# A two-layer graph network: joined attributes, places read at once, a difference on TensorE, one-hots in two parts

## The chip, the cores and the metric
The kernel runs on one core of one Trainium2 chip. The metric is the device time of one execution in microseconds (us). The engines are PE (TensorE), PEld (its weight loads), DVE (VectorE), ACT (ScalarE), POOL (GpSimd) and SP (SyncE, which only issues DMAs here).

## The reference
6250 nodes with 128 features, 106,250 edges sorted by target (a self loop for each node among them). Two layers, each behind a layer norm and a relu, each added to x:

```
# layer 0: attention for each of the 128 channels by itself
a  = f_src[src] + f_dst[dst];  e = where(a >= 0, a, 0.2 * a)
ex = exp(e - segment_max(e, dst)[dst])
out0 = segment_sum(f_v[src] * ex / segment_sum(ex, dst)[dst], dst)
# layer 1: a message, and one weight for each edge (softmax over ALL edges, mean of 8 heads)
scale = mlp(edge_attr_32);  msg = silu(h[src] @ W_node * scale + edge_attr_16 @ W_sh)
alpha = softmax(mlp([h[src][:64], h[dst][:64], edge_attr_32]), axis=0).mean(heads)
out1 = layernorm(h + segment_sum(msg * alpha, dst) @ W_out)
```
Inputs and outputs are float32.

## The kernel before
The sorted edges are cut into 464 pieces of at most 256, each of which belongs to one block of 128 target nodes; two pieces make a **unit** (512 edges), and there are NI = 232 units. For each piece a table in SBUF (`items_row`, int32) holds two places: where its edges begin (off) and at which row its block begins (row); so a unit has four places, side by side.

The stages run one after the other, each a block of instruction streams for the five engines, which meet at its end: `prepare` (table of places, first projections), `layer0_edges`, `node_tables` (quotient, norm, second projections), `layer1_edges`, `layer1_aggregate`, `finish`. The order within a stream is written out by hand; streams wait for each other through semaphores. `run_items` makes a loop of 29 **turns** of eight steps each (U = 8); the first and last turn are written out, the others are a hardware loop. A step works on several units at once: `f(lap, u, d)` is the part f for the unit d places ahead of the step's own.

**The join.** Layer 1 reads, for a unit, 80 rows of one array `ea_d` in DRAM: the 32 attributes twice, and the 16. `prepare` makes it at the end of ACT's stream (L538 to L541) with five DRAM to DRAM copies, in rows of 834 values (3336 bytes); SP in layer 1 waits for the five (`joined`).

**Layer 0's loop** (L790 to L1125), per unit: SP reads the four places with four `value_load`s and issues four loads (marks `lo` and rows of the target block `fd`, two each); it waits until the unit eight before is through (`hold`). POOL gathers 4 x 128 source rows (L856) into G, up to eight units ahead. ACT takes the absolute value of the marks; DVE compares them to one-hots (L1027). PE's `front` (L880, L885) turns G and adds the target part in PSUM; ACT's `bring` copies that to SBUF (L955); DVE's leaky step (L1036). The segment maximum comes from two scans on DVE (`running` L1047, then `back` L1060, backwards), which carry the last column to the next unit through ACT's `link`. DVE's `gap` (L1074) subtracts the maximum, ACT's `exps` (L977) takes exp of 513 columns, PE's `turn` transposes the one-hots (L901) and the result (L908), ACT copies both out (L988, L998), DVE's `weigh` multiplies by the gathered values (L1086) and PE's `collect` sums over edges (16 products, L926). Two units later DVE scales the one node that the unit shares with those before (`scale`, L1100, by column 0 of exp's result) and adds the two halves into SBUF at places that it reads with two `value_load`s (`add`, L1113). DVE's order in a step: leaky(1), scale(-2), running(1), add(-2, first), back(1), add(-2, second), weigh(0), gap(1), onehot(3).

**Layer 1's loop** (L1130 to L1515), per unit: SP reads four places again, then waits for PE's product of four units before (`a1p`) and of eight before (`sh_ready`), then issues six loads (L1222 to L1224). PE's `first` (L1265, L1272, which needs DVE's one-hots L1431, and these the six loads), `inputs`, `attributes`, `second`, `third`, `heads`; ACT's silus; DVE's message.

**Aggregation** (L1520 to L1671), per unit: SP loads the messages, eight units ahead; ACT (3 or 4 parts) and DVE (the odd part, every second unit, L1653) multiply by the weights; DVE makes the one-hot `pick` (512 columns, L1646) two units ahead; PE multiplies (8 products, L1604); DVE adds the two halves (L1667), each at a place that it reads just before. DVE's order: add(0, first), weigh(2) (pick and multiply), add(0, second). The two adds of neighbouring pieces may hit the same columns, so each waits for the one before it (`acc_done`).

Of the kernel before, what the change touches and what calls it, by code (L numbers as in the profile page):

```python
# [20 lines left out]
RADD = bass.bass_isa.ReduceOp.add  # L21

# [76 lines left out]
def build(nc, x, src_pad, dst_pad, ea32, ea16, w0cat, b0cat, w1cat, fc1, b1, fc2, b2, fc3, b3, w_sh,  # L99
          aw1e, ab1, aw2, ab2, aw3, ab3, w_out, out):  # L100
    top = ExitStack()
    with top:
# [17 lines left out]


# [4 lines left out]
        JOINS = (2 * EA + SH) // SH  # L126
# [13 lines left out]
        ident_b = sb("ident_b", [P, P], BF16)  # L140
        local = sb("local", [P, NI * TJ], F32)
# [227 lines left out]
        def prepare():  # L369
# [5 lines left out]
            with st:  # L375
# [60 lines left out]
                with nc.Block() as block:  # L436
# [74 lines left out]
                    def _(act):  # L511
# [26 lines left out]
                        for k in range(JOINS):  # L538
                            rows = ea16 if k == JOINS - 1 else ea32[k * SH % EA:k * SH % EA + SH, :]
                            act.dma_start(ea_d[k * SH:(k + 1) * SH, :].rearrange("a (k e) -> (a k) e", e=EQ),  # L540
                                          rows.rearrange("a (k e) -> (a k) e", e=EQ)).then_inc(joined, 16)  # L541

                    @block.vector
                    def _(dve):
# [62 lines left out]
                        nc.vector.tensor_copy(ident_b[:, :], ident[:, :])  # L607
                        dve.wait_ge(s_w, 32)
# [170 lines left out]
        def layer0_edges():  # L779

            st = ExitStack()
            with st:
# [6 lines left out]
                qe_t = sb("l0_qe", [P, 2, 2, IT + 1], F32, st)  # L789
                q_t, e_t = (qe_t[:, :, k, :] for k in range(2))  # L790
                top_t = sb("l0_top", [P, 2, IT + 1], F32, st)
                w_t = sb("l0_w", [P, R, IT + 2], F32, st)
# [17 lines left out]
                gap_ready = sem("l0_gap_ready", st)  # L810
                w_ready = sem("l0_w_ready", st)
# [9 lines left out]
                with nc.Block() as block:  # L821
                    @block.sync
                    def _(sp):
                        def rows(lap, u, d):
# [3 lines left out]
                            off = [sp.value_load(items_row[0:1, bass.ds(i * 4 + 2 * h, 1)], min_val=0, max_val=OFF_MAX) for h in range(2)]  # L828
                            row = [sp.value_load(items_row[0:1, bass.ds(i * 4 + 2 * h + 1, 1)], min_val=0, max_val=NB * P) for h in range(2)]
# [8 lines left out]

                        def step(lap, u):
                            rows(lap, u, 0)  # L840
                        run_items(sp, step)

# [22 lines left out]
                    def _(pe):  # L865
# [23 lines left out]
                        def turn(lap, u, d):  # L889
# [7 lines left out]
                            wv = w_t[:, g, 1:IT + 1].rearrange("p (j e) -> p j e", j=TJ)  # L897
# [112 lines left out]
                    def _(dve):  # L1010
# [52 lines left out]
                        def gap(lap, u, d):  # L1063

                            i, s, lp = item(lap, u, d)
                            if not exists(i, NI):
                                return
# [763 lines left out]
```

## Time and profile before

| | us |
|---|---|
| median of 3 runs (3906.5 to 3914.71) | 3909.83 |
| profiled execution | 3906.95 |
| its span | 3905.1 |

| engine | busy us | share |
|---|---|---|
| PE | 2844.4 | 73% |
| DVE | 2471.9 | 63% |
| POOL | 1931.8 | 49% |
| ACT | 1884.0 | 48% |

The stages don't overlap, so the shares of the whole span say little: the tables by stage in the rows below are what to read. "Granted clock" is the share of TensorE's full 2.4 GHz that it was given in a stretch; 0.50 is 1.2 GHz. The DMA share is the mean busy share of the core's 16 DMA engines.

### The profile page before, as it was taken

How to read it: one execution, taken by the hardware profiler on the slowest of the kernel's cores; microseconds unless marked ns; L12 is line 12 of the kernel's file. 1: busy time of each engine (PE TensorE's matmuls, PEld its weight loads, DVE VectorE, ACT ScalarE, POOL GpSimd, SP SyncE). 2: the span in 40 equal slices, each digit the busy share in tenths (PEclk: the TensorE clock that was granted, in tenths of full speed). 3: DMA queues.
4: the chain of work that ended last, by engine and by line, in shares of the span. 5: the costliest groups of instructions: out<-in, count | busy, mean ns of one | idle time of the engine just before them, and what ended most of it. 6: DMA issues, size and time to landing. Idle time of an engine off the chain costs nothing. (4 is left out here: it accounts for less than half of the span.)

```text
span 3905.1 us, 86777 instructions
## 1 busy us (share of the span) xinstructions
PE 2844.4 (73%) x18862; PEld 2202.3 (56%) x18862; DVE 2471.9 (63%) x5010; ACT 1884.0 (48%) x3923; POOL 1931.8 (49%) x1957
## 2 busy tenths in 40 slices
PE   1506666666666666646999999999999997676765
PEld 0206666666666666523666666666665664565654
DVE  5509999999999999982444444444444444655556
ACT  6205555445454554443554454554554554545454
POOL 0117777777777777405565566665665662000001
PEclk9759999999999999967999999999999998777777
DMA  3695555545455555225676677676766675344442
GB/s 72 203 322 152 147 146 144 147 144 147 142 148 145 145 146 146 78 67 160 202 202 196 198 199 200 203 203 201 203 198 195 202 203 150 111 116 117 115 118 58
DMA packets 509335, 624.22 MB, mean 160 GB/s; under 512 B 78873, under 2 KB 387605, under 8 KB 508502
## 3 DMA queue, kind: packets, MB, share of 16 engines
q1 hardware_dynamic: 372038, 272.23, 25.6%
q0 software_dynamic: 89088, 243.39, 21.8%
q10 hardware_dynamic: 48016, 106.86, 7.9%
q14 instruction: 173, 1.42, 0.1%
q8 instruction: 20, 0.33, 0.0%
HBM read 534.78 MB, written 121.55 MB: 168 GB/s over the span
## 5 line engine op out<-in xcount | busy, mean ns | idle before, releaser
L1245 POOL DMA_INDIRECT l_G<-rows_d,l_sidx x928 | 885.9, 955 | 542.1 <-DVE l_msg L1454 274.5
L856 POOL DMA_INDIRECT l_G<-rows_d,l_sidx x928 | 996.2, 1073 | 307.7 <-issue 232.0
L1431 DVE TENSOR_SCALAR l_oht<-l_lo,mine_bc 128x256 bf16<-128x256 bf16 x464 | 116.2, 305 | 765.9 <-DMA l_in<-ea_d 764.4
L880 PE MATMUL l_A<-ident,l_G 128*128 128x128 f32 x928 | 165.2, 305 | 551.4 <-DVE l_oht L1027 551.2
L1604 PE MATMUL ag_accp<-ag_msg,ag_pick 128*128 128x128 f32 x1856 | 363.8, 358 | 182.2 <-DVE ag_msg L1653 81.4
L926 PE MATMUL l_accp<-l_ohe,H 128*128 128x128 f32 x3712 | 468.9, 282 | 0.0
L1375 ACT ACTIVATE l_h<-l_H,l_cols 128x512 f32<-128x512 f32 x464 | 318.2, 686 | 296.9 <-PE l_H L1282 219.0
L926 PEld LDWEIGHTS l_accp<-l_ohe,H 128*128 128x128 f32 x3712 | 451.9, 199 | 0.0
L1604 PEld LDWEIGHTS ag_accp<-ag_msg,ag_pick 128*128 128x128 f32 x1856 | 312.5, 255 | 233.6 <-DVE big L1667 156.1
L880 PEld LDWEIGHTS l_A<-ident,l_G 128*128 128x128 f32 x928 | 106.3, 150 | 594.6 <-DVE l_oht L1027 343.4
L1587 ACT ACTIVATE ag_msg<-ag_msg,ag_alpha 128x128 f32<-128x128 f32 x812 | 261.3, 390 | 254.3 <-DMA ag_msg<-msg_d 243.1
L1311 PEld LDWEIGHTS l_SC<-big,l_h 128*128 128x128 f32 x1856 | 249.0, 198 | 143.5 <-issue 143.5
L1393 ACT ACTIVATE l_msg<-l_msg 128x512 f32<-128x512 f32 x232 | 145.7, 628 | 379.9 <-DVE l_msg L1457 379.3
L1047 DVE TENSOR_TENSOR_SCAN l_qe<-l_lo,l_qe 128x512 f32<-128x512 bf16 x232 | 298.2, 1285 | 0.3
L1720 POOL TENSOR_TENSOR fi_O<-fi_O,X 128x1280 f32<-128x1280 f32 x5 | 14.4, 2883 | 570.7 <-DVE fi_O L1778 570.7
L977 ACT ACTIVATE l_w<-l_w 128x513 f32<-128x513 f32 x232 | 146.7, 632 | 284.3 <-DVE l_w L1074 284.3
L955 ACT ACTIVATE l_qe<-l_A 128x512 f32<-128x512 f32 x232 | 138.6, 597 | 298.7 <-PE l_A L885 298.7
L1060 DVE TENSOR_TENSOR_SCAN l_top<-l_lo,l_qe 128x513 f32<-128x513 bf16 x232 | 282.5, 1218 | 0.1
L1323 PE MATMUL l_SHP<-l_win,l_in 16*128 16x128 f32 x1856 | 279.2, 291 | 0.0
L1294 PE MATMUL l_H<-l_h,big 128*128 128x512 f32 x464 | 277.8, 683 | 0.0
L1667 DVE TENSOR_TENSOR big<-big,ag_accp 128x128 f32 x464 | 133.6, 288 | 219.1 <-DVE big L1667 121.8
L1282 PE MATMUL l_H<-l_in,l_win 32*128 32x512 f32 x464 | 268.5, 659 | 0.0
(186 smaller groups left out, 6027.4 us busy)
## 6 DMA issues: line engine op xcount, KB each, us to landing
msg_d<-l_msg ACTq DMA_DIRECT2D x232, 256.0 KB
ag_msg<-msg_d SPq DMA_DIRECT2D x232, 256.0 KB, 2.6
l_fd<-dst_d SPq DMA_DIRECT2D x464, 96.0 KB
l_pd<-dst_d SPq DMA_DIRECT2D x464, 96.0 KB
l_in<-ea_d SPq DMA_DIRECT2D x464, 80.0 KB
ea_d<-in_ea_dram ACTq DMA_DIRECT2D x5, 6672.0 KB, 68.6
l_G<-rows_d,l_sidx POOLq DMA_INDIRECT x1856
l_lo<-mark_d SPq DMA_DIRECT2D x464, 64.0 KB
```

The costliest lines, as they stand in the source:

```text
L856: nc.gpsimd.indirect_dma_start(out=G[:, s, j, :], out_offset=None, in_=rows_d[0][:, :], in_offset=bass.IndirectOffsetOnAxis(ap=sidx[:, hal ...
L880: nc.tensor.matmul(av[:, j, :], G[:, s, j, 0:C], ident[:, :], is_transpose=True, start=(j == 0), stop=False, skip_group_check=True)
L926: last = nc.tensor.matmul(accp[b][:, h, k, :], we_t[:, b, h * HJ + j, k * C:(k + 1) * C], oh_e[:, b, h * HJ + j, :], start=(j == 0), stop= ...
L1047: nc.vector.tensor_tensor_scan(q_t[:, b, 1:IT + 1], lo_t[:, s, 0:IT], e_t[:, b, 1:IT + 1], q_t[:, 1 - b, IT:IT + 1], ALU.min, ALU.max).the ...
L1060: nc.vector.tensor_tensor_scan(top_t[:, b, ::-1], lo_t[:, s, IT::-1], q_t[:, b, ::-1], FAR, ALU.min, ALU.max).then_inc(top_ready, 1)
L1245: nc.gpsimd.indirect_dma_start(out=G[:, s, j, :], out_offset=None, in_=rows_d[1][:, :], in_offset=bass.IndirectOffsetOnAxis(ap=sidx[:, hal ...
L1282: nc.tensor.matmul(H1[:, :], w_in[OF_H, :], in_t[OF_H, s, :], start=True, stop=True).then_inc(h1p, 1)
L1294: nc.tensor.matmul(H2[:, :], w_fc2[:, :], h1_t[:, b, :], start=True, stop=True).then_inc(h2p, 1)
L1323: last = nc.tensor.matmul(SP_[:, j, :], sv[:, j, :], w_in[OF_SH, :], start=True, stop=True)
L1375: nc.scalar.activation(out_t[:, s % 2, :], in_p[:, :], ACT.Silu, bias=cols[:, col:col + 1]).then_inc(ready, 1)
L1587: nc.scalar.activation(mine, mine, ACT.Copy, scale=al[:, bass.ds(i * TJ + j, 1)]).then_inc(shared, 1)
L1604: last = nc.tensor.matmul(accp[b][:, h, :], pick[:, b, j, :], msg_t[:, s, j, :], start=(j % HJ == 0), stop=(j % HJ == HJ - 1))
```

## The change
Four edits.
1. `places` reads a unit's four places with one read of 16 bytes, on SP in both layers' loops, and on DVE (layer 0 and the aggregation), where it takes the place of the two reads for the adds.
2. The five joining copies leave `prepare`. SP's stream in layer 0's loop issues two DMAs for each unit, behind the unit's loads, which join SHARE = 460 columns (80 rows of 1840 bytes); a last pair takes the 32 columns that are left. `joined` is waited for as before.
3. `gap` and `exps` go. PE adds four products of the maximum with minus the identity to the transposed e in PSUM, and ACT takes exp as it copies from there. The one column that `scale` needs is a small exp of its own on ACT (`carry`). e and q are now kept for four units (R = 4) and not for two, w_t goes, and `back` waits for PE's and ACT's use of the maximum of two units before.
4. In the aggregation `pick` is made in two instructions of 256 columns, one behind each add; the read of the next unit's places stands ahead of the second add.

```diff
+        def places(engine, i):
+            _, (off_a, row_a, off_b, row_b) = nc.values_load_multi_w_load_instructions(
+                items_row[0:1, bass.ds(i * 4, 4)], engines=(engine,), min_val=0, max_val=OFF_MAX, ...
+            return (off_a, off_b), (inside(row_a), inside(row_b))
-        JOINS = (2 * EA + SH) // SH
+        SHARE = EP // NI
+        JOINS = 2 * NI + 2
...
-                        for k in range(JOINS):
-                            rows = ea16 if k == JOINS - 1 else ea32[k * SH % EA:k * SH % EA + SH, :]
-                            act.dma_start(ea_d[k * SH:(k + 1) * SH, :].rearrange("a (k e) -> (a k) e", e=EQ),
-                                          rows.rearrange("a (k e) -> (a k) e", e=EQ)).then_inc(joined, 16)
+                        nc.vector.tensor_scalar(minus[:, :], ident[:, :], -1.0, None, ALU.mult)
...  layer 0, SP
-                            off = [sp.value_load(items_row[0:1, bass.ds(i * 4 + 2 * h, 1)], ...) for h in range(2)]
-                            row = [sp.value_load(items_row[0:1, bass.ds(i * 4 + 2 * h + 1, 1)], ...) for h in range(2)]
+                            off, row = places(SP_ENGINE, i)
+                        def join(a, n):
+                            sp.dma_start(ea_d[0:2 * EA, bass.ds(a, n)].rearrange("(r a) e -> r a e", r=2),
+                                         ea32[:, bass.ds(a, n)].unsqueeze(0).to_broadcast([2, EA, n])).then_inc(joined, 16)
+                            sp.dma_start(ea_d[2 * EA:2 * EA + SH, bass.ds(a, n)], ea16[:, bass.ds(a, n)]).then_inc(joined, 16)
                         def step(lap, u):
                             rows(lap, u, 0)
+                            if exists(i, NI):
+                                join(i * SHARE, SHARE)
...  layer 0, PE
-                            pe.wait_ge(w_ready, i + 1)
+                            pe.wait_ge(top_ready, i + 1)
                             for j in range(TJ):
-                                last = nc.tensor.matmul(W[b][:, j, :], wv[:, j, :], ident[:, :], is_transpose=True,
-                                                        start=(j == 0), stop=(j == TJ - 1), skip_group_check=True)
+                                nc.tensor.matmul(W[b][:, j, :], ev[:, j, :], ident[:, :], is_transpose=True,
+                                                 start=(j == 0), stop=False, skip_group_check=True)
+                            for j in range(TJ):
+                                last = nc.tensor.matmul(W[b][:, j, :], tv[:, j, :], minus[:, :],
+                                                        start=False, stop=(j == TJ - 1), skip_group_check=True)
...  layer 0, ACT
-                            act.wait_ge(gap_ready, i + 1)
-                            nc.scalar.activation(w_t[:, g, 0:IT + 1], w_t[:, g, 0:IT + 1], ACT.Exp).then_inc(w_ready, 1)
+                            nc.scalar.activation(front_t[:, g:g + 1], top_t[:, s % 2, 0:1], ACT.Exp, scale=-1.0,
+                                                 bias=e_t[:, g, 0:1]).then_inc(front_ready, 1)
-                            nc.scalar.activation(we_t[:, b, :, 0:C], W[b][:, :, :], ACT.Copy).then_inc(we_ready, 1)
+                            nc.scalar.activation(we_t[:, b, :, 0:C], W[b][:, :, :], ACT.Exp).then_inc(we_ready, 1)
                         def step(lap, u):
-                            exps(lap, u, 0)
                             bring(lap, u, 2)
+                            carry(lap, u, 0)
                             weights(lap, u, 0)
...  layer 0, DVE
+                            if after(i, 2):
+                                dve.wait_ge(wt_ready, i - 1)
+                                dve.wait_ge(front_ready, i - 1)
                             nc.vector.tensor_tensor_scan(top_t[:, b, ::-1], lo_t[:, s, IT::-1], q_t[:, g, ::-1], ...
-                            nc.vector.tensor_tensor(w_t[:, g, 0:IT + 1], e_t[:, b, :], top_t[:, b, :],
-                                                    ALU.subtract).then_inc(gap_ready, 1)
                             running(lap, u, 1)
-                            add(lap, u, -2, 0)
+                            at = places(DVE_ENGINE, i)[1] if exists(i, NI) else None
+                            add(lap, u, -2, 0, at)
                             back(lap, u, 1)
-                            add(lap, u, -2, 1)
+                            add(lap, u, -2, 1, at)
                             weigh(lap, u, 0)
-                            gap(lap, u, 1)
                             onehot(lap, u, 3)
...  layer 1, SP: off, row = places(SP_ENGINE, i) for the four value_loads
...  aggregation, DVE
-                            nc.vector.tensor_tensor(pick[:, b, :, :], iota_row[:, :].unsqueeze(1).to_broadcast([P, TJ, P]), ...
+                            nc.vector.tensor_tensor(pick[:, b, h * HJ:(h + 1) * HJ, :], ...
                         def step(lap, u):
-                            add(lap, u, 0, 0)
+                            if u == 0:
+                                at[0] = where_to(lap, 0)
+                            add(lap, u, 0, 0, at[0])
+                            picks(lap, u, 2, 0)
                             weigh(lap, u, 2)
-                            add(lap, u, 0, 1)
+                            follows = where_to(lap, u + 1) if u + 1 < U else None
+                            add(lap, u, 0, 1, at[0])
+                            at[0] = follows
+                            picks(lap, u, 2, 1)
```

## Rows read from the trace of the kernel before
**Rows 1.** Busy time by stretch: start:end, us, then engines, granted clock, DMA share, GB/s.
```profile
174.00:269.00 95.00, 0.00 (x0) 0.00 (x0) 12.52 (x3) 0.20 (x1) 29.32 (x31) 0.50 0.99 331
...
286.90:1640.00 1353.10, 925.64 (x7818) 854.63 (x7818) 1244.92 (x2300) 679.75 (x1384) 975.77 (x924) 0.93 0.51 143
1814.00:3284.00 1470.00, 1375.76 (x8515) 925.83 (x8514) 643.44 (x1491) 742.35 (x1154) 878.21 (x942) 0.95 0.69 200
3324.00:3842.00 518.00, 363.84 (x1856) 312.48 (x1856) 299.09 (x812) 261.32 (x812) 0.00 (x0) 0.76 0.40 114
```
**Rows 2.** Timeline, start of layer 0 (start, us, engine, line); last, a DMA issue group.
```profile
167.37 3.38 ACTq L540 DMA_DIRECT2D ea_d<-in_ea_dram  x5
...
186.99 0.07 DVE L1012 MEMSET l_lo<- 128x16 bf16 x1
188.05 23.98 SPq L837 DMA_DIRECT2D l_fd<-dst_d  x1
...
286.92 0.69 DVE L1036 SCALAR_TENSOR_TENSOR l_qe<-l_qe 128x512 f32<-128x512 f32 x1
...
ea_d<-in_ea_dram ACTq DMA_DIRECT2D x5, 6672.0 KB, 68.6
```
**Rows 3.** Timeline of DVE, one unit of layer 0's loop.
```profile
1014.18 0.69 DVE L1036 SCALAR_TENSOR_TENSOR l_qe<-l_qe 128x512 f32<-128x512 f32 x1
...
1017.93 0.69 DVE L1086 TENSOR_TENSOR H<-H,l_G 128x512 f32<-128x512 f32 x1
1018.54 0.69 DVE L1074 TENSOR_TENSOR l_w<-l_qe,l_top 128x513 f32<-128x513 f32 x1
1019.14 0.47 DVE L1027 TENSOR_SCALAR l_oht<-l_who,mine_bc 128x256 bf16<-128x256 bf16 x2
1019.53 0.68 DVE L1036 SCALAR_TENSOR_TENSOR l_qe<-l_qe 128x512 f32<-128x512 f32 x1
```
**Rows 4.** Timeline of PE, ACT and DVE, one unit of layer 0's loop.
```profile
1007.12 0.77 DVE L1086 TENSOR_TENSOR H<-H,l_G 128x512 f32<-128x512 f32 x1 [0.71 <-issue]
...
1008.98 0.66 PE L880 MATMUL l_A<-ident,l_G 128*128 128x128 f32 x4 [0.49 <-DVE l_oht L1027]
...
1010.35 0.61 PE L908 MATMUL l_W<-ident,l_w 128*128 128x128 f32 x4
...
1010.79 1.95 PE L926 MATMUL l_accp<-l_ohe,H 128*128 128x128 f32 x16
...
1010.99 0.60 ACT L998 ACTIVATE H<-l_W 128x512 f32<-128x512 f32 x1
```
**Rows 5.** Groups by line, POOL's gathers in layer 0: busy, mean ns, idle before them.
```profile
L856 POOL DMA_INDIRECT l_G<-rows_d,l_sidx x928 | 996.2, 1073 | 307.7 <-issue 232.0 <-DVE H L1086 52.7 <-POOL l_sidx L853 23.1
```
**Rows 6.** Timeline of SP, layer 1: one unit's loads and the next unit's first.
```profile
2340.32 0.33 SPq L1222 DMA_DIRECT2D l_lo<-code_d  x1
...
2342.94 0.33 SPq L1224 DMA_DIRECT2D l_in<-ea_d  x1
2346.33 0.34 SPq L1222 DMA_DIRECT2D l_lo<-code_d  x1
```
**Rows 7.** Layer 1: a wait in total, one such wait, granted clock behind it.
```profile
PE l_A L1272 <- DVE l_oht L1431: 97.0, 73, 6.2
...
2373.81 0.83 PE L1272 MATMUL l_A<-l_oht,l_pd 128*128 128x256 bf16 x6 [1.74 <-DVE l_oht L1431]
...
2376.00:2378.00 2.00, 2.00 (x6) 1.26 (x6) 0.00 (x0) 1.09 (x2) 1.39 (x3) 0.50 0.58 127
```
**Rows 8.** Timeline of the aggregation: adds and a pick on DVE, products on PE.
```profile
3563.65 0.29 DVE L1667 TENSOR_TENSOR big<-big,ag_accp 128x128 f32 x1 [0.66 <-DVE big L1667]
3563.85 0.68 DVE L1646 TENSOR_TENSOR ag_pick<-iota_row,local 128x512 f32<-128x512 f32 x1
...
3565.84 0.29 DVE L1667 TENSOR_TENSOR big<-big,ag_accp 128x128 f32 x1 [0.65 <-DVE big L1667]
...
3611.87 2.07 PE L1604 MATMUL ag_accp<-ag_msg,ag_pick 128*128 128x128 f32 x8 [1.17 <-DVE ag_pick L1646]
```

More of the change, by code:

```diff
@@ L21 @@
 RADD = bass.bass_isa.ReduceOp.add
+SP_ENGINE = mybir.EngineType.SP
+DVE_ENGINE = mybir.EngineType.DVE
 P = 128
@@ L119, in dram, with inside @@
             return nc.dram_tensor(name, shape, dt).ap()
+        def places(engine, i):
+            _, (off_a, row_a, off_b, row_b) = nc.values_load_multi_w_load_instructions(
+                items_row[0:1, bass.ds(i * 4, 4)], engines=(engine,), min_val=0, max_val=OFF_MAX,
+                skip_runtime_bounds_check_because="the table on the chip is clamped to the arrays when it is built")
+            def inside(v):
+                return nc.s_assert_within(v, 0, NB * P,
+                                          skip_runtime_bounds_check_because="blocks are counted up to NB when the table is built")
+            return (off_a, off_b), (inside(row_a), inside(row_b))
         chunk_d = dram("chunk_d", [HG * P], F32)
@@ L952, in bring @@
                             act.wait_ge(a_ready, i + 1)
-                            if after(i, 2):
-                                act.wait_ge(gap_ready, i - 1)
-                            nc.scalar.activation(e_t[:, s % 2, 1:IT + 1], A[s % 2][:, :], ACT.Copy).then_inc(a_copied, 1)
+                            if after(i, R):
+                                act.wait_ge(wt_ready, i - R + 1)
+                            nc.scalar.activation(e_t[:, s % R, 1:IT + 1], A[s % 2][:, :], ACT.Copy).then_inc(a_copied, 1)
                         def link(lap, u, d):
@@ L961, in link, with carry @@
                                 return
[L962 removed]
                             act.wait_ge(q_ready, i + 1)
[L964 to L967 removed]
+                            if after(i, R - 1):
+                                act.wait_ge(front_ready, i - R + 2)
+                            nc.scalar.activation(qe_t[:, (s + 1) % R, :, 0:1],
+                                                 q_t[:, s % R, IT:IT + 1].unsqueeze(1).to_broadcast([P, 2, 1]),
                                                  ACT.Copy).then_inc(linked, 1)
[L970 removed]
+                        def carry(lap, u, d):
                             i, s, lp = item(lap, u, d)
@@ L1213, in rows @@
                                 return
-                            off = [sp.value_load(items_row[0:1, bass.ds(i * 4 + 2 * h, 1)], min_val=0, max_val=OFF_MAX) for h in range(2)]
-                            row = [sp.value_load(items_row[0:1, bass.ds(i * 4 + 2 * h + 1, 1)], min_val=0, max_val=NB * P) for h in range(2)]
+                            off, row = places(SP_ENGINE, i)
                             if after(i, R):
@@ L1522, in layer1_aggregate @@
             SHARED = [sum(OWN[0:s + 1]) for s in range(U)]
-            PICKED = [sum(1 + TJ - n for n in OWN[0:s + 1]) for s in range(U)]
+            PICKED = [sum(2 + TJ - n for n in OWN[0:s + 1]) for s in range(U)]
             st = ExitStack()
@@ L1636, in _, with picks @@
                         al = alpha[:, (HEADS - 1) % 2, :]
-                        def weigh(lap, u, d):
+                        def picks(lap, u, d, h):
                             i, s, lp = item(lap, u, d)
```

73 lines of the change are left out of this document (34 added, 39 removed).

## The prediction
> **What bounds the kernel now.** I read the times by stage first, because no single engine is busy all the way: the page puts PE at 73% and DVE at 63% of the span. [rows 1] gives four stretches: 95 us in which PE does nothing and the DMA engines are 0.99 busy; layer 0's loop, 1353.1 us, DVE busy 1244.9 of it (92%), PE 68%; layer 1's loop, 1470 us, PE busy 1375.8 (94%), DVE 44%; the aggregation, 518 us, where no engine passes 71%. Each has its own limit.
>
> *Start of layer 0* [rows 2]: ACT issues five copies that join the attributes at 167.4 us, in front of the block's end. SP's small loads for the first units then take up to 23.98 us to issue. DVE's zeroing is over at 187.06 us, but the first leaky step runs at 286.92. The limit is the joining copies, whose data layer 0 never reads.
>
> *Layer 0's loop*: the timeline of DVE over one unit [rows 3] has no idle time; a unit takes 1019.53 - 1014.18 = 5.35 us. The mean over the loop is 1353.1/231 = 5.86, since DVE idles 108 us, 3.7 us at each turn of eight units.
>
> *Layer 1's loop*: PE is nearly full, but the timeline of SP [rows 6] shows who paces it. SP starts a unit's six loads at 2340.32 and the next unit's at 2346.33: 6.01 us, of which the six issues take 2340.32 to 2343.27 = 2.95 and the other 3.06 hold four reads of places and two waits. The list of waits has no wait of SP on a product in this loop, so SP isn't held back by anyone: it is the pace. PE feels it [rows 7]: 97.0 us of waiting for the one-hots, which wait for the loads; and after a wait of 1.74 us the granted clock drops to 0.50 (1.2 GHz) for some 7 us.
>
> *Aggregation* [rows 8]: add, pick, (multiply,) add. The add at 3563.65 was idle 0.66 us behind the add before it, though that takes only 0.29: between them stands a read of a place into a register, and nothing is queued to cover it.
>
> **The change, part by part.** The sum is made against the profiled execution, 3906.95 us (span 3905.1, 1.85 around it); the median of the runs is 3909.83, 2.9 above.
>
> *Joining moved into layer 0's loop.* Without the copies at the front, the first leaky step follows the zeroing after the one-hots (0.5 us), PE's front (1008.98 to 1010.35 = 1.4 at full clock [rows 4], double at 1.2 GHz) and ACT's copy (0.6): some 4 us. The block also ends earlier by ACT's 3.38 us of issuing. 187.06 - 3.4 + 4 = 188 against 286.92: **-99 us**. Nothing else holds it: loads and gathers issue from about 170. Bounds: -95 (the stretch with idle PE) to -105.
> The price is paid in the loop. SP issues two more DMAs per unit, each 0.33 us and some 0.5 from start to start (2.95/6): 1.0 us, while three reads go. SP is held by DVE in this loop, so this lies beside. On the engines: the join is 5 x 6672 KB = 34.2 MB [rows 2], which at the 331 GB/s of the first stretch [rows 1] is 103 us of all 16 engines, or 1650 engine-us. Spread over all 16 that is 0.08 of the loop on top of 0.51, and loads are issued eight units ahead. I cost it at 15 us; 0 and, if it falls on few engines, the rival below are the ends.
>
> *Layer 0's difference on TensorE.* The subtraction (L1074) goes: the next instruction now starts 0.60 us after it (1018.54 to 1019.14) [rows 3], and DVE has no idle: 231 x 0.60 = -139 us if nothing else is late. PE gets four f32 products of 128x128; sixteen take 1.95 us (L926) [rows 4], so 0.49 a unit. PE's unit is now 1008.98 to 1012.74 = 3.76; 4.25 is under DVE's new 4.75. The dependent chain: front's start to the start of ACT's weights is 1008.98 to 1010.99 = 2.01, to become 2.50, plus an Exp of about 0.63; ready 3.13 us after front. DVE comes to its weighted product 1017.93 - 1014.18 = 3.75 after leaky, about 3.6 after front: hidden by about 0.5 us at full clock. Once a turn it is not: at 1007.12 that instruction already waits 0.71 us at the low clock, and the four products then cost twice, 0.98: 28 x 1.0 = +27. ACT loses a 0.63 us Exp and gains one of one column (0.2): off the path. The new waits of back (wt_ready, front_ready, two units old) have been met a step before; behind them on DVE only its own next add queues.
> POOL is next in line: its 928 gathers take 996.2 + 232.0 + 23.1 = 1251 us with what stands between them [rows 5], some of it made by following DVE. DVE alone would come to 1353 - 139 + 27 = 1241. The two, each halting at its own turns, don't overlap perfectly; I add 19. With the 15 for DMA: 1353 -> 1275, **-78 us**. Ends: 0 (POOL no faster than now) and -139.
>
> *One read for four places, SP.* In layer 1 three of four reads go. If the 3.06 us were all reads, each is 0.77 and 2.3 us go; if the two waits and their increments took 0.3 each (POOL's issue gaps are 232.0/928 = 0.25), 0.6 and 1.8. SP's unit falls to 3.7 to 4.2 us. PE is then the pace. Its floor: 1375.8 busy less the loss at low clock, 1470 x (1 - 0.95) = 74, is 1302 us, 5.61 a unit. So 94 us of idle and 74 of slow clock, 168 in all, are there to be had. What is late next are turns of DVE, ACT and POOL, today covered by waiting for SP; I leave a sixth: **-140 us**. Ends: -50 (half the waits of 97 remain as other waits and the clock keeps falling) and -168.
> The Trainium skill has two rules for such a read: a floor of some 600 ns ("DMA: Bandwidth & Descriptors", Latency and other measured facts), with which the lower value above agrees, and some 200 ns per register even in bulk ("Runtime: NRT & Kernel Launch", Instruction fetch mechanics). By the second the four-place read costs an estimated 0.8 us: it changes nothing on SP, but DVE's read in the aggregation would be 0.2 us longer, 232 x 0.2 = 46 us of the next term. No row here shows a read of four.
>
> *Aggregation: picks in two parts, one read.* Of a unit's 2.19 us with a multiply (3563.65 to 3565.84) the 0.66 behind the second add goes: half a pick is there, and the place is read earlier. The instructions alone: two adds 0.20 from start to start, two half picks 0.69 + 0.08 for the second start, a multiply in half of the units 0.14: 1.31 us. The read now stands ahead of the second add, covered by half a pick; uncovered it would be 0.66. 1.31 to 1.97; I take 1.7. But the mean granted clock here is 0.76 [rows 1], so half the time is at 1.2 GHz, where a unit's eight products take 2.07 us [rows 8]: PE paces that half at about 2.15. With 0.07 for the turns: 2.0 against 518/232 = 2.23, **-55 us**. Ends: +10 (DVE waits as long before the second add, plus the extra start) and -125.
>
> Sum: 99 + 78 + 140 + 55 = 372; 3906.95 - 372 = **3535 us**.
>
> **Rivals.**
> *The joins fall on two engines, 28%.* The destination's slowest dimension in the first of the two DMAs is 2 (the repeat). If rows are dealt out by it, two engines carry 4/5 of the join: 1650 x 0.8/2 = 660 us each, beside the 0.51 x 1353 = 690 that they carry now: 1350, less if two engines alone copy quicker than sixteen together, in a loop I put at 1275. They run full, every load and gather waits for its part on them, and the loop gives all of its 78 us back and a little more: 3535 + 85 = 3620. Against: nothing in the trace shows a DMA on two engines. The Trainium skill states just this dealing ("DMA: Bandwidth & Descriptors", Why a DMA increments its semaphore by 16 and not by 1); no run here shows it yet.
> *Layer 1 keeps its pace, 14%.* Something else halts PE at each turn and the clock still drops. For: the long waits come at the same place of each turn. Against: SP, which waits for nobody here, is behind in every unit. Layer 1 gives 40 instead of 140: 3635.
> *More than forecast, 10%.* In the aggregation shorter gaps hold PE at the high clock, 1.65 us a unit (-80 more), and layer 1 gives all 168: 3535 - 80 - 28 = 3427.
> *Slower, 4%.* One engine carries 4/5 of the join, 1320 us beside its 690: layer 0's loop takes 2010 us, +657; with the other terms (-294) 4270 us. For it speaks as little in the trace as for two. It decides once the fullest engine's part of the join passes 1353 + 294 - 690 = 957 us.
>
> **Numbers.** Forecast 44%: 3535, by itself 3480 to 3590. Joins on two engines 28% (3620), layer 1 as before 14% (3635), more 10% (3427), slower 4%. The range 3455 to 3670 holds the first three. About 0.2% (8 us) is what a measurement tells from no change: faster 0.95, same 0.01, slower 0.04.
>
> **What would show it.** DVE's first leaky step near 188 us; layer 0's unit 4.75 us within a turn, with PE 4.25; PE's wait for one-hots in layer 1 under 20 us and the clock 0.98 or more, SP waiting for PE there; the aggregation's idle between adds gone, a shorter one before the second add. Wrong: DMA share near 1 on a few engines, late loads in layer 0, or POOL's gathers without waits there; layer 1's clock still 0.95.

## The result, and the profile after

The changed kernel takes 3428.57 us (median of 4 runs, 3423.26 to 3430.77) against 3911.08 us of the kernel before on the same chip: ratio 0.8765, 95% interval 0.875 to 0.878. 3535 was forecast, and the range began at 3455. The profiled execution has a span of 3427.6 us, 477.5 less than before.

Busy time of the changed kernel by stretch, columns as in [rows 1]: end of the start, layer 0's loop, layer 1's loop, aggregation.

```profile
92.00:188.00 96.00, 53.34 (x156) 27.44 (x157) 58.70 (x93) 24.95 (x67) 14.74 (x16) 0.80 0.55 156
189.30:1522.50 1333.20, 1119.35 (x9649) 1052.44 (x9648) 1108.85 (x2068) 570.98 (x1384) 1032.10 (x940) 0.95 0.63 171
1690.00:2945.00 1255.00, 1247.38 (x8516) 866.69 (x8516) 651.38 (x1493) 712.72 (x1151) 906.58 (x948) 0.99 0.81 235
2987.80:3364.00 376.20, 266.21 (x1856) 226.83 (x1856) 299.62 (x1042) 260.27 (x809) 0.00 (x0) 0.99 0.55 156
```

PE is full in layer 1 (1247.4 of 1255 us); in layer 0 no engine is: PE 84%, DVE 83%. The aggregation's clock went from 0.76 to 0.99. From the first start to the last start of one instruction in each stage (leaky step; first product of the attributes; add), with the time from the launch to the first leaky step in the first row:

| stage | before | after | difference | forecast |
|---|---|---|---|---|
| start of layer 0 | 286.9 | 189.3 | -97.6 | -99 |
| layer 0's loop | 1352.5 | 1333.2 | -19.3 | -78 |
| layer 1's loop | 1467.0 | 1247.1 | -219.9 | -140 |
| aggregation | 514.5 | 373.6 | -140.9 | -55 |

Start of layer 0, timeline of DVE (beside [rows 2]): the wait that stood for the joins is 2.69 us.

```profile
185.64 0.97 DVE L1055 TENSOR_SCALAR l_oht<-l_who,mine_bc 128x256 bf16<-128x256 bf16 x4
189.30 0.69 DVE L1064 SCALAR_TENSOR_TENSOR l_qe<-l_qe 128x512 f32<-128x512 f32 x1 [2.69 <-ACT l_qe L979]
```

Layer 0, groups by line: GpSimd's gathers (beside [rows 5]), PE's first products of a unit, and the products with the negated identity.

```profile
L876 POOL DMA_INDIRECT l_G<-rows_d,l_sidx x928 | 1037.2, 1118 | 299.6 <-issue 267.4 <-POOL l_sidx L873 23.1 <-DVE H L1102 9.1
...
L900 PE MATMUL l_A<-ident,l_G 128*128 128x128 f32 x928 | 158.1, 295 | 240.6 <-DMA l_G<-rows_d,l_sidx 187.7 <-DVE l_oht L1055 44.1 <-issue 2.1
...
L932 PE MATMUL l_W<-minus,l_top 128*128 128x128 f32 x1856 | 258.9, 285 | 0.0
```

Here the 59 missing microseconds stand. Busy and idle of the gathers make 1037.2 + 299.6 = 1336.8 us, as long as the whole loop: they run without a wait from 169.0 to 1515.4 us, and PE now waits 187.7 us for gathered rows. GpSimd paces layer 0, and a gather got longer, 1073 to 1118 ns. The idle time that the rows put down to DVE (52.7 us before, 9.1 now) is no wait: it is 171 and 30 gathers with the usual 0.30 us ahead of them. The real waits for DVE stood ahead of the copies of the indices, once in eight units, which [rows 5] does not show: 44.9 us in the loop before (L853), 0.1 now (L873). The products with `minus` are two records each: 1856 records for 928 products.

Layer 1, the list of waits (in total, times, longest) and a group by line: SP, which waited for nobody, now waits for PE, 354.2 us in 226 waits, 1.57 us each; PE waits 3.9 us for one-hots where [rows 7] has 97.0.

```profile
SPq L85 <- PE l_A L1298: 354.2, 226, 2.6
...
L1287 PE MATMUL l_A<-l_oht,l_pd 128*128 128x256 bf16 x1392 | 191.2, 274 | 3.9 <-DVE l_oht L1446 3.9
```

The aggregation's adds, group by line: idle 76.6 us ahead of them (219.1 in the kernel before).

```profile
L1691 DVE TENSOR_TENSOR big<-big,ag_accp 128x128 f32 x464 | 132.1, 285 | 76.6 <-PE ag_accp L1619 42.1 <-issue 26.1 <-DVE big L1691 0.5
```

### The profile page after: what moved, and what is told of

The parts are those of the page before. It is cut to its first block and busy times, and to the rows that moved or that the text cites. A ratio compares the mean times of both kernels' runs of the same rounds, so it can differ in the third digit from the quotient of the medians.

```text
span 3427.6 us, 83570 instructions
## 1 busy us (share of the span) xinstructions
PE 2819.4 (82%) x20718; PEld 2260.0 (66%) x20718; DVE 2347.8 (68%) x5011; ACT 1746.5 (51%) x3923; POOL 1995.6 (58%) x1957
## 5 line engine op out<-in xcount | busy, mean ns | idle before, releaser
L876 POOL DMA_INDIRECT l_G<-rows_d,l_sidx x928 | 1037.2, 1118 | 299.6 <-issue 267.4
L1260 POOL DMA_INDIRECT l_G<-rows_d,l_sidx x928 | 908.3, 979 | 330.5 <-issue 255.4
L950 PE MATMUL l_accp<-l_ohe,H 128*128 128x128 f32 x3712 | 454.7, 276 | 0.0
L950 PEld LDWEIGHTS l_accp<-l_ohe,H 128*128 128x128 f32 x3712 | 436.5, 193 | 0.0
L1456 DVE TENSOR_TENSOR big<-l_SC,l_b 128x512 f32<-128x512 f32 x232 | 160.3, 691 | 355.6 <-PE l_SC L1326 355.3
L1619 PE MATMUL ag_accp<-ag_msg,ag_pick 128*128 128x128 f32 x1856 | 266.2, 289 | 140.0 <-DVE ag_pick L1661 130.4
L900 PE MATMUL l_A<-ident,l_G 128*128 128x128 f32 x928 | 158.1, 295 | 240.6 <-DMA l_G<-rows_d,l_sidx 187.7
L1619 PEld LDWEIGHTS ag_accp<-ag_msg,ag_pick 128*128 128x128 f32 x1856 | 226.8, 193 | 179.4 <-DVE big L1691 124.3
L1102 DVE TENSOR_TENSOR H<-H,l_G 128x512 f32<-128x512 f32 x232 | 159.7, 689 | 215.1 <-issue 185.4
L1298 PE MATMUL l_A<-l_in,l_win 32*128 32x512 f32 x464 | 261.8, 644 | 0.0
L932 PE MATMUL l_W<-minus,l_top 128*128 128x128 f32 x1856 | 258.9, 285 | 0.0
L1309 PE MATMUL l_H<-l_h,big 128*128 128x512 f32 x464 | 256.3, 634 | 0.0
```

Of the source, the lines that this page charges most:

```text
L876: nc.gpsimd.indirect_dma_start(out=G[:, s, j, :], out_offset=None, in_=rows_d[0][:, :], in_offset=bass.IndirectOffsetOnAxis(ap=sidx[:, hal ...
L900: nc.tensor.matmul(av[:, j, :], G[:, s, j, 0:C], ident[:, :], is_transpose=True, start=(j == 0), stop=False, skip_group_check=True)
L950: last = nc.tensor.matmul(accp[b][:, h, k, :], we_t[:, b, h * HJ + j, k * C:(k + 1) * C], oh_e[:, b, h * HJ + j, :], start=(j == 0), stop= ...
L1260: nc.gpsimd.indirect_dma_start(out=G[:, s, j, :], out_offset=None, in_=rows_d[1][:, :], in_offset=bass.IndirectOffsetOnAxis(ap=sidx[:, hal ...
L1298: nc.tensor.matmul(A1[:, :], w_in[OF_A, :], in_t[OF_A, s, :], start=False, stop=True, skip_group_check=True).then_inc(a1p, 1)
L1619: last = nc.tensor.matmul(accp[b][:, h, :], pick[:, b, j, :], msg_t[:, s, j, :], start=(j % HJ == 0), stop=(j % HJ == HJ - 1))
```

## The experiments

The theory at first: in layer 0 the gathers set the pace (G), in layer 1 SP's reads did (S), in the aggregation the reads between the adds (R). Times are medians of 4 runs; ratios are against the kernel before, measured beside them (3903 to 3912 us), with their 95% intervals. The runs stood on several chips, which shifts a difference of two times by up to 9 us; the ratios are less touched by that. "Loop" is layer 0's, from the first leaky step to the last in the trace.

### What paces layer 0

**a1_spread_joins**: the two-engine rival.
```
-  ea_d[0:2 * EA, ...].rearrange("(r a) e -> r a e", r=2), ea32[...].unsqueeze(0).to_broadcast([2, EA, n])
+  ea_d[0:2 * EA, ...].rearrange("(r a) e -> a r e", r=2), ea32[...].unsqueeze(1).to_broadcast([EA, 2, n])
```


> The changed kernel, with the join of the 32 attribute rows written as attribute-major (32 rows, each to its two places) instead of copy-major (2 copies of 32 rows), the same bytes. In the changed kernel layer 0's loop took 1333 us where 1275 was forecast, and TensorE waits 188 us there for the gathered rows to land. Theory J (the joins get in the gathers' way, because a transfer whose slowest dimension is 2 is dealt to few of the DMA engines): the loop falls to about 1285, the whole from 3428 to about 3380. Theory G (GpSimd's own pace of issuing four gathers a unit sets the loop): same time, 3420 to 3435, and the wait for the gathered rows stays at 170 us or more. Theory P (TensorE, whose maximum products cost 1.06 us a unit where 0.49 was forecast): same time too.


3425.14 us, ratio 0.877 (0.8749 to 0.8791); loop 1328.3. The order of the joins' rows gains nothing that can be told. To how many DMA engines either form goes, no trace here shows.

**a2_join_in_prepare**: `join` out of layer 0's SP stream, the five copies back at the end of ACT's stream.


> The changed kernel with one part undone: the attributes are joined at the start, by ScalarE's queue, as in the kernel before; nothing is joined in layer 0's loop. The start gets 98 us longer in every theory. Theory J (the joins in the loop delay the gathers): the loop falls from 1333 to about 1280, so the whole is about 3475. Theories G (GpSimd's issue pace) and P (TensorE's price): the loop stays at 1325 to 1335, the whole is 3520 to 3530.


3521.40 us, 0.9022 (0.9006 to 0.9039). The start is 96 us longer, the loop 1324.3: the joins cost the loop 9 us. J falls.

**a3_top_turned**: PE's price.
```
-  nc.tensor.matmul(W[b][:, j, :], tv[:, j, :], minus[:, :], start=False, ...)
+  nc.tensor.matmul(W[b][:, j, :], tv[:, j, :], ident[:, :], is_transpose=True, start=False, ...)
```


> The changed kernel with the running maximum turned by a transpose with the plain identity instead of multiplied by the negated one, so that a sum stands in the place of the difference (the weights are then not the reference's): TensorE gets rid of the doubled price of four products a unit (1.06 us to about 0.5). Theory P (the products' price is what keeps layer 0 at 1333 us instead of 1275): the loop falls by 40 to 58 us, the whole to 3370 to 3390. Theory G (the gathers' pace sets the loop): under 10 us in all, TensorE waits longer for the gathered rows (from 188 to about 240 us).


3430.75 us, 0.8778 (0.8762 to 0.8794); loop 1334.7. The same products as transposes are 928 records and 151.8 us instead of 258.9, and PE's wait for gathered rows grows from 187.7 to 269.3 us. P falls: 107 us of PE, and not one of the time.

**a4_three_gathers**: `for j in range(TJ - 1)` around the gather; the fourth gather of each unit is left out.


> The changed kernel with the fourth gather of each unit of layer 0 left out (the fourth tile holds a constant, so a quarter of the gathered rows is missing; all the work of the other engines stays). Theory G (gathers set the pace): TensorE's wait for the gathered rows goes, the loop falls from 1333 to the 4.76 us of VectorE's unit, 1270 to 1280, the whole to 3370 to 3380. Theory P (TensorE's price): the loop stays within 10 us of 1333. If both hold at once the loop falls by about half of it.


3256.09 us, 0.834 (0.8326 to 0.8354). Layer 0's loop, then its gathers:
```profile
191.20:1346.70 1155.50, 1076.37 (x9650) 1013.96 (x9648) 1104.97 (x2068) 567.07 (x1385) 822.78 (x708) 0.99 0.64 171
...
L878 POOL DMA_INDIRECT l_G<-rows_d,l_sidx x696 | 826.4, 1187 | 295.6 <-issue 149.9 <-DVE H L1106 122.7 <-POOL l_sidx L875 23.0
```
G holds, and by more than supposed: the loop falls by 178 us, to 5.0 us a unit, and GpSimd now waits for DVE, up to 3.2 us at a time (of the 122.7 us in 178 places some 53 are the usual 0.30). DVE and PE, with three quarters of the gathers, run the new layer 0 in 1155 us.

**c1_layer0_of_before**: the functions of layer 0 from the kernel before, joins at the start.


> The changed kernel with the whole of layer 0's loop, and the joins at the start, as in the kernel before; layer 1 and the aggregation stay changed. Layer 0's loop took 1352.5 us in the kernel before and 1324 with its new form and the joins at the start (3521 us in all). If the stages add up: 3521 + 28 = 3550 us, 3543 to 3557: then taking 0.6 us a unit (139 us) off VectorE earned 28 us, because the gathers set the pace. If layer 0 weighs on the stages behind it: outside that.


3545.28 us, 0.9067 (0.9036 to 0.9099); loop 1349.9. Against a2 all of layer 0's edits but the join are worth 24 us (25.6 in the loop, 18 by the ratios).

### What lengthens the gathers

Timeline of GpSimd and DVE in the changed kernel: many gathers take 0.95 us, but this one, begun 0.29 us after the forward scan, takes 1.75.

```profile
864.24 1.28 DVE L1074 TENSOR_TENSOR_SCAN l_qe<-l_lo,l_qe 128x512 f32<-128x512 bf16 x1
864.53 1.75 POOL L876 DMA_INDIRECT l_G<-rows_d,l_sidx  x1 [0.30 <-issue]
...
865.44 0.39 DVE L1128 TENSOR_TENSOR big<-big,l_accp 128x256 f32 x1
```

I first blamed the add: queued behind the scan by now that the place is read early, it would hold GpSimd off while it waits (W).

**e1_adds_wait_for_scans**
```
+  dve.wait_ge(q_ready, n + 1)      # n: the unit just scanned
   add(lap, u, -2, 0, at)
   back(lap, u, 1)
+  dve.wait_ge(top_ready, n + 1)
   add(lap, u, -2, 1, at)
```


> Layer 0's loop was found to be paced by GpSimd's gathers (mean 1.118 us and 0.30 between them, four a unit). In the trace of the changed kernel a gather that begins 0.29 us after the forward scan takes 1.75 us instead of 0.95, and it ends 0.44 us after the first add on VectorE. This kernel adds one wait ahead of each of the two adds, on the scan that VectorE has just been given. Theory W (an add that stands queued behind a scan already holds GpSimd off, so that the hold lasts as long as the scan's rest and the add): the gathers' mean falls to 1.02 to 1.05, the loop from 1333 to 1260 to 1290 us, the whole from 3428 to 3355 to 3385. Theory X (only the add's own 0.39 us holds GpSimd off, or something else does): mean 1.10 or more, the two waits cost VectorE some 0.15 us a unit, the whole 3425 to 3445.


3376.56 us, 0.8651 (0.8633 to 0.8668); loop 1274.8, gathers' mean 1054 ns. Two waits made the kernel 52 us faster (45 by the ratios).

**e2_adds_side_by_side**: leaky, running, scale, add, add, back, weigh, onehot.


> The changed kernel with VectorE's order in layer 0 changed: leaky step, forward scan, scale, first add, second add, backward scan, so that each add waits on a semaphore of the instruction just ahead of it and none is queued behind a scan. Theory W: as with the waits, the gathers' mean 1.02 to 1.06, the whole 3355 to 3395. Theory X: two adds one after the other hold GpSimd for some 0.7 us together, the gathers' mean stays at 1.10 or more, the whole 3420 to 3450.


3394.95 us, 0.8696 (0.868 to 0.8713); loop 1297.6, mean 1077 ns.

**e3_one_column_adds**: `mine[:, :, 0:1]` and `accp[...][:, h, :, 0:1]` in the add.


> The changed kernel with each add of layer 0 cut to one column of the 128 (the rest of the products is not added up; everything else stays). Theory A (the adds are what lengthens the gathers, waiting or running): the gathers' mean falls from 1.118 under 1.05, the loop by 60 us or more, the whole under 3370. Theory O (the one-hots and the transfers lengthen them): the mean stays above 1.09 and the whole within 15 us of 3428. If the part that is queued behind the scan is what counts, not the running, the gain is small here and large in the run with the waits.


3366.91 us, 0.8625 (0.8609 to 0.8641); loop 1261.6, mean 1041 ns.

**e4_waits_and_whole_pick**: e1 with the aggregation's one-hots in one instruction (b3 below).


> A version that may beat the changed kernel: the two waits ahead of layer 0's adds, and the aggregation's one-hots in one instruction (which alone took 47 us off). Theory W: 3382 less 45 to 75, 3305 to 3340. Theory X: 3380 to 3400.


3332.27 us, 0.853 (0.8514 to 0.8546): the two gains add up.

The times of e1, e2 and e4 fall where W had put them, though e2's mean (1077) is above W's 1.06 and e3, in which W expected less than e1's gain, gained more (62 against 52 us). W is wrong: with the waits the long gather is still there:

```profile
852.42 1.28 DVE L1074 TENSOR_TENSOR_SCAN l_qe<-l_lo,l_qe 128x512 f32<-128x512 bf16 x1
852.83 1.62 POOL L876 DMA_INDIRECT l_G<-rows_d,l_sidx  x1 [0.30 <-issue]
853.83 0.42 DVE L1128 TENSOR_TENSOR big<-big,l_accp 128x256 f32 x1
```

It ends at 854.45, which is 2.03 us after the scan's start; in the changed kernel 864.53 + 1.75 - 864.24 = 2.04. I sorted the gathers of 400 to 1200 us by their start after the forward scan's start, to the nearest 0.2 us (the rows 0.6 and 1.0 are left out; means of each group):

| gather begins after scan | changed: mean us (count), end after scan's start | e1 | e3 | f1 (below) |
|---|---|---|---|---|
| 0.0 | 0.95 (25), 0.98 | 0.95 (107), 0.98 | 0.95 (62), 1.00 | 0.95 (47), 0.99 |
| 0.2 | 1.74 (64), 2.02 | 1.82 (1), 2.04 | 1.62 (20), 1.84 | 0.95 (42), 1.22 |
| 0.4 | 1.63 (10), 2.04 | 1.62 (3), 2.04 | 1.63 (15), 2.04 | 0.95 (26), 1.41 |
| 0.8 | 1.18 (5), 2.04 | 1.28 (10), 2.06 | 1.22 (8), 2.04 | 0.95 (10), 1.78 |
| 1.2 | 0.95 (28), 2.18 | 0.95 (83), 2.22 | 0.95 (39), 2.21 | 0.95 (36), 2.20 |

The end at 2.04 us, 0.76 after the scan's own end, is the same with a whole add behind the scan, a one-column add, or a wait; the kernel before has it too. The backward scan has the same tail: 2.73 + 0.76 = 3.49 in the changed kernel (109 gathers end there, at 3.49 to 3.52), 2.97 + 0.76 = 3.73 in e1 (3.73 to 3.75). So it is the scan, and the waits only shifted the two rhythms so that more gathers begin outside its window (at 0.0 and at 1.2: 190 instead of 53). The theory now (S in the expectations of f1 and f2): an instruction of DVE with two inputs in SBUF holds up a gather that begins under it.

The gathers' time is the loop's: against the changed kernel their mean times 928 falls by 59 us in e1, 38 in e2 and 71 in e3, the loop by 58, 36 and 72.

**f1_scan_from_psum**: the leaky step writes into PSUM, the scan reads that, and one more copy of ACT (`e_back`) brings it back for PE.
```
-  scalar_tensor_tensor(out=e, in0=e, scalar=SLOPE, in1=e, ...)
+  scalar_tensor_tensor(out=A[s % 2][:, :], in0=e, scalar=SLOPE, in1=A[s % 2][:, :], ...)
-  tensor_tensor_scan(q_t[...], lo_t[:, s, 0:IT], e_t[:, g, 1:IT + 1], ...)
+  tensor_tensor_scan(q_t[...], lo_t[:, s, 0:IT], A[s % 2][:, :], ...)
```


> The changed kernel, with layer 0's leaky step writing its result into PSUM, the forward scan reading it there, and ScalarE bringing it back to SBUF by one more copy a unit: the forward scan and the leaky step then have one input in SBUF each instead of two. Theory S (a gather that begins under a VectorE instruction with two inputs in SBUF is held until some 0.76 us after that instruction's end): gathers that begin 0.2 to 1.0 us after the forward scan take 0.95 us and no longer end at 2.04 us after its start; the mean falls from 1.118 to 1.02 to 1.07, the loop to 1260 to 1300 us, the whole from 3428 to 3355 to 3395. Theory R (the scan holds GpSimd off wherever its inputs lie, or the read of the places behind it does): the ends stay at 2.04 us and the mean at 1.10 or more, the whole 3420 to 3450.


3340.44 us, 0.8538 (0.8516 to 0.8561), below the range that the theory gave; loop 1245.1, gathers' mean 1025 ns. The same moment as above, 0.28 us after a forward scan, and further on 0.28 us after a backward scan, which still has both inputs in SBUF:

```profile
864.82 1.28 DVE L1085 TENSOR_TENSOR_SCAN l_qe<-l_lo,l_qe,l_A 128x512 f32<-128x512 bf16 x1
865.10 0.95 POOL L877 DMA_INDIRECT l_G<-rows_d,l_sidx  x1 [0.30 <-issue]
...
877.32 1.22 DVE L1101 TENSOR_TENSOR_SCAN l_top<-l_lo,l_qe 128x513 f32<-128x513 bf16 x1
877.60 1.69 POOL L877 DMA_INDIRECT l_G<-rows_d,l_sidx  x1 [0.30 <-issue]
```

One scan lost its hold, the other kept it (877.60 + 1.69 - 877.32 = 1.97, 0.75 after its end). The leaky step, whose second input moved to PSUM too, is a second witness. First the changed kernel, 0.20 us after its start, then f1, 0.22 us after:

```profile
1019.97 0.68 DVE L1064 SCALAR_TENSOR_TENSOR l_qe<-l_qe 128x512 f32<-128x512 f32 x1
1020.17 1.30 POOL L876 DMA_INDIRECT l_G<-rows_d,l_sidx  x1 [0.30 <-issue]
```
```profile
541.50 0.68 DVE L1075 SCALAR_TENSOR_TENSOR l_A<-l_qe,l_A 128x512 f32<-128x512 f32 x1
541.72 0.95 POOL L877 DMA_INDIRECT l_G<-rows_d,l_sidx  x1 [0.30 <-issue]
```

The other instructions of DVE fit. `weigh`, with both inputs in SBUF in every kernel, holds gathers in f1 too: of those that begin under it, 0.15 us or more after its start, none ends less than 0.81 us after its end. Under the adds, with one input in PSUM, and the one-hots, with one tile as input, a gather takes 0.95 (25 of them in f1). `gap`, with both inputs in SBUF, held gathers in the kernel before; this one begins 0.23 us after the `gap` of [rows 3], at 1018.54:

```profile
1018.77 1.27 POOL L856 DMA_INDIRECT l_G<-rows_d,l_sidx  x1 [0.30 <-DVE H L1086]
```

What all 928 gathers take beyond 0.95 us, in us, by the last instruction that DVE had begun before each:

| kernel | forward scan | backward scan | `gap` | leaky | `weigh` | in all | loop |
|---|---|---|---|---|---|---|---|
| before | 27 | 20 | 56 | 9 | 3 | 115 | 1352.5 |
| changed | 104 | 34 | - | 10 | 8 | 156 | 1333.2 |
| f1 | 0 | 58 | - | 0 | 13 | 70 | 1245.1 |

From the changed kernel to f1 the holds fall by 86 us and the loop by 88. The change took away the 56 us under `gap` and got 91 more under the scans; why the gathers now begin under the forward scan more often was not tested.

The Trainium skill has this rule ("SBUF — State Buffer", Who interferes with whom): an instruction of VectorE with two inputs in SBUF contends with one of GpSimd that reads SBUF, since its second input comes through the shared read interface. The trace agrees, in the two scans above: 0.95 us with one input in SBUF, 1.69 with two.

**f2_psum_and_whole_pick**, **f3_psum_waits_whole_pick**: f1 with the aggregation's one-hots in one instruction (b3 below), and that with e1's waits.


> The same with the aggregation's one-hots in one instruction (47 us less there). Theory S: 3310 to 3350. Theory R: 3375 to 3405.

> The same with the two waits ahead of layer 0's adds as well. If the waits helped only by moving the phase between VectorE's unit and the gathers (4 x 1.25 = 5.0 us at best), they add little here: within 25 us of the kernel without them, of either sign. If they free GpSimd by themselves, as first supposed: 40 to 60 us less than it.


3298.37 us, 0.8424 (0.8407 to 0.8441), and 3317.90 us, 0.8483 (0.8469 to 0.8497). With the forward scan out of the way the waits cost 19.5 us: they free nothing by themselves. f2's range, 3310 to 3350, was missed on the same side as f1's. **f2 beats both kernels**, by 3.9% against the changed one (0.8424 / 0.8765 = 0.961).

### Layer 1

**b1_l1_four_reads**: the four `value_load`s back in layer 1's SP stream. **b2_before_l1_one_read**: in the kernel before, `off, row = places(SP_ENGINE, i)` there and nothing else.


> The changed kernel with one part undone: in layer 1, SyncE reads a unit's four places one by one again. Theory S (SyncE's cycle with four reads set layer 1's pace before, all 217 us that the stage lost come from the one read): layer 1 back to about 1466 us, the whole 3428 + 217 = 3645. Rival (part of the 217 us comes from elsewhere, at most the 168 of my bound from the read): 3570 to 3600.

> The kernel before with one part done: only layer 1's SyncE reads the four places at once. Theory S: layer 1 from 1466 to about 1250, the whole from 3903 to about 3686. Rival: the gain stops at 140 to 168 us, 3735 to 3763, with TensorE's clock in layer 1 still under 0.97.


b1 3647.81 us, 0.9331 (0.9303 to 0.9359); b2 3689.55 us, 0.9431 (0.9414 to 0.9448). Layer 1's stretch, first b1, then b2:
```profile
1689.20:3159.80 1470.60, 1374.20 (x8504) 923.92 (x8504) 641.72 (x1490) 742.33 (x1151) 878.66 (x941) 0.95 0.69 199
```
```profile
1815.90:3062.60 1246.70, 1243.92 (x8504) 864.65 (x8504) 650.91 (x1490) 712.07 (x1151) 903.30 (x942) 1.00 0.82 235
```
The one read is worth 219 to 221 us, from both sides: SP's cycle with four reads was the whole of layer 1's loss.

But `places` does two things, and no run takes them apart. Each `value_load` also checks at run time that the place is within its bounds, and `places` leaves that check out (`skip_runtime_bounds_check_because`, which the diff above does not show). The records of SP's stream in layer 1, kernel before (L1214 is two of the four reads), then changed (count: shortest/median/longest ns):

```profile
L1214 SPq TENSOR_LOAD <-items_row x460: 260/275/1164, 1816.0 to 3270.3; - x154
L1214 SPq SEQ_ASSERT  x460: 18/18/18, 1816.5 to 3270.8; - x154
```
```profile
L125 SPq TENSOR_LOAD <-items_row x231: 294/298/320, 1692.3 to 2921.4; - x116
```

In one unit of the kernel before, the four reads take 2445.11 to 2447.85 = 2.74 us, 0.69 each, of which some 0.3 us behind each load are the check; the read of four takes 0.41 us (2221.05 to 2221.46) and has none. So of the 2.3 us that SP saves, some 1.2 may be the checks and 1.1 the three reads (an estimate from these records). By it, four reads without checks would bring SP to 6.0 - 1.2 = 4.8 us a unit, already under PE's 5.40: leaving out the checks alone might have earned most of the 220 us. That was not run.

### The aggregation

**b3_agg_whole_pick**
```
-  picks(lap, u, 2, 0) ... picks(lap, u, 2, 1)       # 2 x (HJ x P) columns
+  picks(lap, u, 2)                                  # TJ x P columns, ahead of weigh
```


> The changed kernel with the aggregation's one-hots in one instruction again (ahead of the multiply), and the one read kept: tells the split from the read, which together took 142 us off that stage (a unit 2.23 to 1.62 us). Theory R (the reads between adds were the cost; the split only gives the next add a cover): at most +30 us, 3430 to 3460. Theory H (the split matters as much: with nothing between the second add and the next first one, TensorE's products come late and its clock falls): +60 to +140, 3490 to 3570.


3381.64 us, 0.8648 (0.863 to 0.8665): 47 us *faster* than with the split. Neither theory had that sign.

**b4_agg_two_reads**: `at = dve.value_load(...)` ahead of each add, one-hots in two parts.


> The changed kernel with the split one-hots kept, but a read of one place ahead of each add again. Theory R: each read costs 0.66 less the 0.34 of the half pick that now covers it, some 0.3 a read, 0.6 a unit: +100 to +140 us, 3530 to 3570. Theory H: the half picks hide most of both reads, +0 to +40.


3598.83 us, 0.9196 (0.9179 to 0.9213): +170. The one-hots and the adds by line and the stage's stretch, of b3, then of b4:
```profile
L1661 DVE TENSOR_TENSOR ag_pick<-iota_row,local 128x512 f32<-128x512 f32 x232 | 159.5, 687 | 0.1
L1691 DVE TENSOR_TENSOR big<-big,ag_accp 128x128 f32 x464 | 133.3, 287 | 47.0 <-DVE big L1691 16.6 <-PE ag_accp L1619 2.8
...
2974.00:3305.60 331.60, 267.45 (x1848) 225.07 (x1847) 286.18 (x809) 257.63 (x802) 0.00 (x0) 0.99 0.64 177
```
```profile
L1661 DVE TENSOR_TENSOR ag_pick<-iota_row,local 128x256 f32<-128x256 f32 x464 | 194.5, 420 | 0.1
L1692 DVE TENSOR_TENSOR big<-big,ag_accp 128x128 f32 x464 | 133.6, 288 | 237.5 <-issue 155.0 <-PE ag_accp L1619 80.0 <-DVE big L1692 2.0
...
2991.40:3541.80 550.40, 381.51 (x1848) 327.39 (x1847) 314.37 (x1039) 257.97 (x801) 0.00 (x0) 0.71 0.38 107
```
Reading late keeps 237.5 us of idle time ahead of the adds, and the clock goes to 0.71. The read (with its check left out, as above) is the whole gain: with the one read the stage takes 331.2 us with whole one-hots, 373.6 with split ones, 550.1 with split ones and two reads, 514.5 before. The split costs DVE 299.6 - 286.2 = 13 us of busy and (376.2 - 299.6) - (331.6 - 286.2) = 31 us of idle time. That the second part pulls the adds of neighbouring units apart is my reading of it; no run tests it.

## Why the prediction was wrong, point by point

- *Joining moved*: -99 forecast, -97.6 at the start; in the loop 15 forecast, 9 measured (a2). Right. The rival of two engines, to which I gave 28%, has lost its price: the joins cost the loop 9 us in all, and writing them the other way changes 3428.6 to 3425.1. Whether the rows go to two engines stays open. Issuing a unit's two joins takes SP 0.82 and 0.59 us, not 0.33 each; it stayed off the path.
- *Layer 0's difference*: the step that failed is "POOL is next in line: 1251 us, some of it made by following DVE". POOL became the pace, and its own stream is longer than that sum. I left out the 52.7 us "for DVE", which are ordinary spaces, and the 29 copies of indices, some 10 us: with them the old row gives 996.2 + 307.7 + 10 = 1314. Then the gathers grew: 1.118 us where 1.073 stood, 928 x 0.045 = 41 us, since more of them began under a scan. Together 1037.2 + 299.6 + 10 = 1347 us, of which some 20 lie ahead of the loop. The lower end of the term, 0 ("POOL no faster than now"), was nearer than the value I took. The four products were mis-sized: I took L926's sixteen records for sixteen products, but they are eight (and L1604's eight are four), so it is 1.06 us a unit and not 0.49. It cost nothing (a3). DVE alone, 1241 in my working, is at most 1155 (a4). I had kept the kernel before's idle time at the turns; in a4 DVE idles 1155.5 - 1105.0 = 51 us where it idled 108, and what shortened these halts was not tested.
- *One read on SP*: mechanism right, term mis-sized: 220 instead of 140, beyond my end of 168. SP's own cycle is 5.40 - 1.57 = 3.8 us, as forecast (3.7 to 4.2), in part because the checks went, which I had not counted apart. The 0.8 us that I had as the second figure for a read of four is not borne out: 0.41 on SP, 0.47 on DVE (3100.19 to 3100.66). The floor for PE was wrong: busy time less the loss at the low clock gave 1302, but PE runs the stage in 1247 when nothing holds it. A busy PE that is fed late shows more busy time than the clock alone explains; what part of it are waits inside the modelled ends is open. The sixth that I held back was unfounded: nothing else was late, and the rival in which layer 1 keeps its pace (14%) is out.
- *Aggregation*: "PE paces that half at about 2.15" failed. The low clock left with the halts, and comes back with them (b4, 0.71): 1.62 us a unit (373.6/231), clock 0.99. My estimate for DVE alone, 1.7, was near. The read was under its cover, but the split was no part of the gain and took 42 us of it back.
- *More than forecast* (10%, 3427) came within 2 us of the time, partly by chance: it gave 80 us more to the aggregation (86 measured) and 28 more to layer 1 (80 measured), and layer 0's missing 59 make up the rest. Its mechanism in the aggregation was right; it should have had more than 10%, since the change removed the very halts that stood ahead of the low clock.

What each part is worth in the end: joins moved 93 us (a2), layer 0's other edits 24 (c1), the read in layer 1 219 (b1), the aggregation 141, of which the read gives 183 (514.5 - 331.2) and the split takes 42 (373.6 - 331.2).

## What to carry to other kernels

Where an engine is freed, add up the whole stream of the next engine, gaps included, and don't discount it for waits unless their row shows them: divide an idle time by its count first, for 52.7 us in 171 places were no wait. A low clock and a long busy time that come from halts leave with the halts: for a floor use the time of the instructions at full clock. A read of places into registers costs by the read and its run-time check, not by the place; do it once, early, and put each part to the test by itself, the check and the "cover" too.

## What the runs showed of the hardware that I had not expected

- A gather takes 0.95 us of GpSimd and 0.30 to the next; one that begins 0.2 to 1.0 us after the start of a scan with two inputs in SBUF ends 0.75 to 0.76 us after the scan's end, up to 0.9 us late. With the scan's second input in PSUM it takes 0.95. The same holds of the leaky step, `gap` and `weigh`, with some 0.82 us behind their end. A semaphore wait elsewhere on DVE can win or lose 20 to 50 us merely by moving that phase (e1, f3).
- Four reads of one place with their run-time checks take SP 2.74 us, some 0.39 for a read and 0.3 for its check; a read of four places without a check takes 0.41.
- A float32 product with 128x128 of plain data is two records and 1.06 us for four; as a transpose with the identity it is one record and about 0.61.
